# A ternary feed-forward stage: second products over fourteen steps, transposes through one PSUM bank, residuals at step 14

## The reference

```
z  = layernorm(x)
zq = clip(round(z * 127/max|z|), -128, 127) / (127/max|z|)       # per token
h  = zq @ ternary(w1)^T                                          # 512 -> 2048
y  = w[0]*h[s-1] + w[1]*h[s] + w[2]*h[s+1] + b                   # depthwise, along tokens
g  = silu(y)
gq = clip(round(g * 127/max|g|), -128, 127) / (127/max|g|)       # per token
x  = x + gq @ ternary(w2)^T                                      # 2048 -> 512
```

## Time and profile before

| | us |
|---|---|
| median of 3 executions | 1597.73 |
| lowest and highest | 1594.97 and 1601.06 |
| the profiled execution's own time | 1597.53 |
| its span in the trace | 1595.7 |
| first matmul of batch 0 of the feed-forward | 187.61 |
| first matmul of batches 1, 2, 3, 4 | 234.29, 276.39, 323.09, 372.60 |
| last matmul group of the feed-forward starts | 580.26 |

### The profile page before, as it was taken

The page is one execution under the profiler, slowest core; times in us unless marked ns, Lnnn a source line. Parts: engine busy times, 40 slices in busy tenths (PEclk is TensorE's granted clock), DMA queues, the critical chain, the costliest instruction groups (busy, mean ns, idle before and its releaser), DMA issues. The chain is left out here.

```text
span 1595.7 us, 28021 instructions
## 1 busy us (share of the span) xinstructions
PE 1476.2 (93%) x8732; PEld 657.1 (41%) x8732; DVE 1230.3 (77%) x1469; ACT 1109.7 (70%) x1894; POOL 1058.7 (66%) x765
## 2 busy tenths in 40 slices
PE   6999877999999987899999999999999988999998
PEld 3555433444444443334343434343434323344443
DVE  4999998989889785677676768777777768887763
ACT  6677598888888764666676766666766665667563
POOL 4778537766877645667666767776776665766762
PEclk9999999999999998999999999999999989999999
DMA  8321000000000014121211212121211112222321
GB/s 324 129 86 67 0 1 1 1 1 1 0 0 1 1 67 117 38 59 37 56 39 39 58 33 58 35 57 39 59 36 36 40 54 53 53 53 69 89 53 53
DMA packets 91702, 79.49 MB, mean 50 GB/s; under 512 B 45792, under 2 KB 71264, under 8 KB 91104
## 3 DMA queue, kind: packets, MB, share of 16 engines
q1 hardware_dynamic: 88656, 69.87, 15.8%
q10 hardware_dynamic: 2960, 8.62, 1.4%
HBM read 37.40 MB, written 8.39 MB: 29 GB/s over the span
## 5 line engine op out<-in xcount | busy, mean ns | idle before, releaser
L1652 DVE TENSOR_REDUCE s_mx<-bank 128x2 f32<-128x1024 f32 x248 | 291.7, 1219 | 159.9 <-PE bank L1787 159.1
L1521 ACT ACTIVATE s_E<-bank 128x512 f32<-128x512 f32 x512 | 281.3, 597 | 165.0 <-PE bank L1805 164.0
L1402 POOL TENSOR_TENSOR s_E<-s_E 128x1024 f32<-128x1024 f32 x126 | 300.0, 2392 | 79.5 <-ACT s_E L1521 78.7
L1805 PE MATMUL bank<-s_QA,s_KA 97*128 97x512 f16 x512 | 164.6, 385 | 17.4 <-DVE s_mx L1652 9.9
L1813 PE MATMUL bank<-s_E,s_V 128*32 128x512 f32 x1024 | 139.0, 615 | 4.1 <-ACT s_E L1521 2.3
L2023 POOL TENSOR_TENSOR sm_cx<-m_xf,sm_cx 128x512 f16<-128x512 f32 x60 | 86.3, 1451 | 54.5 <-ACT sm_cx L2080 54.5
L1141 PE MATMUL bank<-f_w2q,w2raw 128*128 128x512 f16 x512 | 121.8, 379 | 0.6 <-DVE w2raw L993 0.3
L815 POOL TENSOR_TENSOR sm_wkv<-sm_wkv,sm_cx 128x511 f32<-128x511 f32 x48 | 66.2, 1380 | 81.8 <-DVE sm_wkv L1005 80.1
L1118 PE MATMUL bank<-sm_zz,w1raw 128*128 128x512 f16 x256 | 99.7, 389 | 22.0 <-DVE sm_cx L1005 13.7
L1656 DVE RECIPROCAL bank<-bank 128x256 f32<-128x256 f32 (+1 forms) x66 | 112.7, 1708 | 9.1 <-PE bank L1821 5.4
L809 POOL TENSOR_TENSOR w1raw<-w1raw,sm_cx 128x512 f32<-128x512 f32 x88 | 115.8, 1337 | 2.3 <-ACT sm_cx L897 2.3
(11 more groups left out here) (288 smaller groups left out, 4065.9 us busy)
## 6 DMA issues: line engine op xcount, KB each, us to landing
sm_cx<-in_ctx SPq DMA_DIRECT2D x16, 768.0 KB, 4.6
X<-in_x SPq DMA_DIRECT2D x8, 1024.0 KB, 6.5
s_QA<-sm_cx SPq DMA_DIRECT2D x256, 32.0 KB, 1.9
out_x<-X SPq DMA_DIRECT2D x8, 1024.0 KB, 4.3
s_KA<-sm_cx SPq DMA_DIRECT2D x249, 32.0 KB, 1.9
w1raw<-in_w ACTq DMA_DIRECT2D x1, 4096.0 KB, 14.3
w2raw<-in_w ACTq DMA_DIRECT2D x1, 4096.0 KB, 28.5
s_QA<-s_qkh SPq DMA_DIRECT2D x128, 32.0 KB, 1.9
```

The source lines that it names most:

```text
L1402: e.tensor_tensor(into, into, other, ALU.add).then_inc(s_sum.sem, 1)
L1521: e.activation(E[:, SLOT[k] + h, :], s_bank(u, nxt)[:, :], ACT.Exp, scale=1.0 / float(np.sqrt(DH)))\
L1652: e.tensor_reduce(mx[:, 2 * i:2 * i + 2, q], MAXED[i][:, :, :], AX.X, ALU.max).then_inc(s_red.sem, 1)
L1805: e.matmul(s_bank(u, nxt)[:, :], KA[0:MROW + 1, m, h, t * P:(t + 1) * P], QA[0:MROW + 1, m, h, :], start=True, stop=True).then_inc(s_sc.se ...
```

## The change

`SECOND` now runs from 16 to 29, one tile a step but for two steps with two. So all of a batch's second product stands in steps 0 to 13 of the batch after next in the interleaving (b-2), and none in steps 14 and 15. `SCALED` moves tiles 8 to 15 one to two steps later. All four chunk transposes go into `AB`, in steps 8, 9, 11 and 12 (`TURN_AT`), with ScalarE's `high` and VectorE's `low` of the same chunk in the same steps; a chunk after the first waits for `low` of the one before it (`s_zl`) where it waited for a residual before. The four residuals of batch b-2 stand together in step 14. The pieces of the diff are, in order, the tables and banks, GpSimd after its steps, ScalarE in a step and after them, VectorE in a step and after them, and TensorE. After batch 7, GpSimd has six scalings in place of four, ScalarE and VectorE one rounding more each, and TensorE begins with tile 0.

```
-        SCALED = (7, 8, 8, 9, 10, 10, 11, 12, 13, 14, 15, 15, 16, 17, 18, 19)
-        SECOND = (15, 16, 16, 17, 18, 18, 19, 20, 20, 21, 21, 22, 23, 23, 24, 25)
+        SCALED = (7, 8, 8, 9, 10, 10, 11, 12, 14, 15, 16, 17, 18, 19, 20, 21)
+        SECOND = (16, 17, 18, 19, 20, 21, 22, 22, 23, 24, 24, 25, 26, 27, 28, 29)
+        TURN_AT = (8, 9, 11, 12)
...
-        zbank = lambda c: OB[c - 1] if c else AB
...
-            for r in (12, 13, 14, 15):
+            for r in range(10, KF):
                 scaled(B - 2, 0, r)
...
-                        for c in in_step(lambda c: (10, 11, 11, 12)[c] if c < KD else -1, j):
-                            high(b + 1, 1 - odd, c, zbank(c))
+                        if j in TURN_AT:
+                            high(b + 1, 1 - odd, TURN_AT.index(j), AB)
...
-            for r in (10, 11, 12, 14):
+            for r in (8, 10, 11, 12, 14):
                 whole(B - 2, 0, r)
...
-                    if has_c and j in (8, 9):
-                        residual(b - 2, odd, 2 * (j - 8))
-                        residual(b - 2, odd, 2 * (j - 8) + 1)
                     if ahead or extra:
-                        for c in in_step(lambda c: (11, 11, 12, 12)[c] if c < KD else -1, j):
-                            low(b + 1, 1 - odd, c, zbank(c))
+                        if j in TURN_AT:
+                            low(b + 1, 1 - odd, TURN_AT.index(j), AB)
+                    if has_c and j == 14:
+                        for q in range(TT):
+                            residual(b - 2, odd, q)
...
+            whole(B - 2, 0, 9)
             whole(B - 2, 0, 13)
             whole(B - 2, 0, 15)
...
-            def linear2(b, r, split=False):
+            def linear2(b, r):
                 if r == 0:
                     s_res.wait(e, b, 0)
-                    if split:
-                        s_zl.wait(e, b + 2, KD)
                     unshift()
...
-            def transposed(b, c, has_c, extra):
+            def transposed(b, c, extra):
                 if c == 0:
                     (s_z if extra else s_r2).wait(e, b, TT)
                     s_s2b.wait(e, b - 1, 0)
-                elif has_c:
-                    s_res.wait(e, b - 3, c)
-                chunk(e, b, c, zbank(c))
+                else:
+                    s_zl.wait(e, b, c)
+                chunk(e, b, c, AB)
...
-                    if has_a:
-                        for r in in_step(lambda r: SECOND[r], j):
-                            linear2(b - 1, r, ahead or extra)
                     if not has_a and j == 15:
                         e.wait_ge(s_wq, 1)
-                        s_zl.wait(e, b + 1, 1)
+                        s_zl.wait(e, b + 1, KD)
...
-                        for c in in_step(lambda c: (10, 11, 12, 12)[c] if c < KD else -1, j):
-                            transposed(b + 1, c, has_c, extra)
+                        if j in TURN_AT:
+                            transposed(b + 1, TURN_AT.index(j), extra)
...
-            for r in range(1, 13):
+            for r in range(13):
                 linear2(B - 2, r)
```

## The result

The changed kernel takes **1634.62 us** (median of four runs, 1631.68 to 1635.97) beside 1596.51 for the kernel before (1594.97 to 1601.06): a ratio of **1.0231, 95% interval 1.0216 to 1.0247**. The forecast has 20 of the 38 us; 18 want an explanation. In two of the kernels further down (chunks at 8 to 11, unshift in step 1) one execution of four ran far longer than the others (3333 and 2205 us); their ratios leave it out, and without it their medians would be 0.4 and 0.2 us lower.

A forecast was written before the change was run, and what follows sets the result against it. TensorE sets the pace, VectorE close behind. Batch 0 +6.2, batch 1 and entry +4.2, five loop batches +6.4, tail +3.4: 20.2 us on 1597.5, forecast 1618 us, range 1607 to 1627.

The forecast's parts named there:

- What bounds the kernel: Feed-forward batches before the change: TensorE sets the pace, busy 45.69 of 46.70 us in batch 2, with VectorE close behind.
- the purely TensorE work of 45.5 us: Batches 2 and 3 before the change: each leaves 45.5 us of TensorE work once its waits are taken off.
- The hand-off through AB: Step 12: TensorE's last chunk waits for chunk 2's low half, 10.1 against 8.2 us, a wait of 1.9 replacing 1.17.
- Clock: the rival dismissed at 0.05: Rival, chance 0.05: every new wait of about 1.9 us is followed by half clock, adding about 30 us: 1648.
- Sum of the loop: Five batches from linear1(14) of batch 2 to that of batch 7: 49.2 us each where it was 47.9, +6.4 us.
- The residuals at step 14: The next batch's unshift in step 0 waits 1.8 us for the last residual, replacing 1.97 in odd batches only.
- linear1(5) at 0: VectorE's queue up to the next batch's step 2: linear1(5) just finds its taps done, cost 0, up to 0.3 a batch.
- the old waits going: Waits before the change, at linear1(14), in step 4 and at odd batches' ends, of 1.17, 0.84 and 1.97, are replaced or go.
- Batch 0: Chunk 0, moved to step 8, makes TensorE stand 8 us with half clock behind: +6.2 us, bounds 3.5 and 8.5.
- Batch 1 and the entry: From linear1(10) of batch 1 to linear1(14) of batch 2: +4.2 us, bounds 2 and 5.
- The tail: Behind batch 7 the unshift waits 3.5 us for the residuals: +3.4 us, bounds 2.5 and 6.2.
- The faster rival: Rival, chance 0.05: no wait is left in the loop, five batches save 12 us, some 1590 us in all.

The follow-up runs named there:

- chunks at 8 to 11: Kernel with tile 3's rounding in step 12, chunks turned in steps 8 to 11, chunk 2's copies ahead of the reduction: 1616.76 us.
- unshift in step 1: Kernel with tile 3's rounding in step 12, unshift and tile 0's product moved from step 0 to 1, tiles 8 and 9 scaled one step later: 1626.85 us.
- the split ones: Kernels with VectorE's big reduction split in two: with tile 3's rounding in step 12, 1615.56 us; also batches 0 and 1 as before, 1608.62; kernel before, 1604.40.
- the last experiment: Changed kernel with GpSimd's scalings of tiles 4 and 5 in step 11 in place of step 10: 1634.51 us.
- the kernel with batches 0 and 1 as before: Changed kernel with the input transposes of batches 0 and 1 in the steps and banks of the kernel before: 1625.28 us.
- the moved rounding: Changed kernel with VectorE's rounding of tile 3 moved from step 10, ahead of the big reduction, to step 12: 1619.00 us.
- the added matmuls: Changed kernel with eight useless 128x512 matmuls added in each step 12, ahead of the wait for chunk 2's low half: 1624.16 us.

## Why the prediction was wrong, point by point

- **What bounds the kernel, and the purely TensorE work of 45.5 us.** Right. Batch 2 after is 48.40 - 2.95 of waiting = 45.45.
- **The hand-off through AB: the step that failed.** Its terms were counted rightly but one: the rounding at 0.34 (0.42 busy) was taken from the earlier trace rows, where GpSimd's scaling started just behind it. The walk shifted VectorE against GpSimd and kept the price. It measured 1.47, 1.05 more, in batch 2, and 1.30 to 1.53 in batches 3 to 6. The chunk waits of the five batches (3 to 7) are 4.3 us above the count for it. With the price restored the wait was 1.74 as counted.
- **Clock: the rival dismissed at 0.05.** For the five batches it was 7.8 us, the largest single part of the miss; the sum had put it at nothing. The reason given was that the waits were 1.9 and 1.8; at 2.8 the reason was gone, and the range had no room for an error of one microsecond in a wait that then costs three more. By its letter (every new wait followed by half clock) the rival was wrong too: no wait of 1.62 to 1.80 was followed by it.
- **Sum of the loop.** 4.3 + 7.8 + the forecast's 6.4 = 18.5 against 18.1 measured; 0.4 is not placed.
- **The residuals at step 14, linear1(5) at 0, the old waits going.** Right: 1.8 by distance, nothing at linear1(5), none of the earlier trace rows left.
- **Batch 0.** 8.7 against 6.2, just over its bound of 8.5. The wait of 8.03 and the half clock behind it are as forecast. Missed was the next one: at 232.60, in step 12, the last chunk waits 4.05 for the low half of the one before it, and a second stretch of half clock behind it costs up to 1.7. The hand-off's 8.2 us for TensorE has three products in it, 2.6 us, and batches 0 and 1 have none; without them the count gives 4.5 where the loop has 1.9.
- **Batch 1 and the entry.** 6.1 against 4.2, over its bound of 5. The last chunk of batch 1 waits 4.39, not 1.9, again for want of the products, with half clock for 7 us around its end (2.7 outside the wait). Against that, the waits of 1.16, 0.73 and 1.66 that the kernel before has in steps 9, 10 and 14 of batch 1 are gone. The wait of chunk 1 for chunk 0's low half is 2.07 where the forecast had 1.9. The wait at batch 2's first matmul did not fall away as forecast, 1.10 of 1.72 is left, and batch 2 adds the 1.05 of the rounding.
- **The tail.** 4.6 against 3.4, within its bounds; the wait is 3.41 as counted (3.5), with 1.7 of half clock behind.
- **The faster rival** priced a batch without waits at 45.5. The runs show more than its own argument against it: even with the chunk's wait removed (2.2 to 3.4 us won where 8 to 16 were expected), the boundary took much of it over.

## What to carry to other kernels

When an edit shifts one engine against another, look up the price of each short VectorE instruction again by what GpSimd will be doing at that moment. And look whether the trace of before already holds a second price for the same instruction; here it held 0.42 and 1.35. Ahead of an engine that is 91 to 93% busy a new wait is not worth its length: ask what it becomes if it is a microsecond longer, and give the half-clock case its own room in the range. And where the second engine is busy for 42 to 45 of 48 us, a wait removed at one place was mostly found again at the next in these runs, so the sum over a batch tells more than any one wait.

## What the runs showed of the hardware

- A 128x512 fp32 rounding on VectorE takes 0.42 us when it is alone or begins first, and 1.30 to 1.53 when a GpSimd tensor-tensor of 1.3 us began 0.05 to 0.3 us ahead of it. The reduction took 4.41 us with GpSimd busy for 1.28 of them (batch 0) and with GpSimd busy for all of them (batch 2 of the kernel before).
- The clock does not follow the length of a wait alone. In the feed-forward it never fell behind a wait below 2.04 us and always fell around one of 3.59 or more. Between these it went both ways. It fell behind 2.04, 2.11, 2.29, 2.33, 2.56, 2.68 and 2.85, and stayed at 2.4 GHz behind 2.06 or 2.07 at chunk 1 of batch 1 in all eight kernels that have this wait, behind 2.35 and 2.40 in the split ones, 2.66 at 341.36 of the last experiment and 2.79 in the changed kernel. Waits of 2.83 did both. The longest without half clock is at the first matmul of batch 2 in the kernel with batches 0 and 1 as before, 3.44 us, with a window behind it:

```profile
275.46 0.39 PE L1121 MATMUL bank<-sm_zz,w1raw 128*128 128x512 f16 x1 [3.44 <-DVE sm_cx L1007]
...
276.50:283.00 6.50, 6.50 (x31) 2.94 (x30) 5.98 (x6) 5.95 (x10) 3.02 (x3) 1.00 0.00 0
```

- A stretch of half clock lasted about 3.4 or 7 us, at a cost of up to 1.7 or 3.4, less what of it lay within the wait. What decides between all these outcomes is open. The Trainium skill, "TensorE: Matmul & The Clock Gate", section "What's actually happening", says that the activity monitor runs freely and not in step with the kernel; waits of like length with unlike outcomes agree with that, and no run here tests it.
- The same wait of 2.49 or 2.50 us in batch 0, with the same instructions ahead of it, left the clock at 1.00 in nine kernels, the one before among them, while five others, among them those with the moved rounding and with the added matmuls, had 3.4 us of half clock there, though none of them is changed in that batch up to that point.
